# Scores of a cross-attention block: rounded queries and their rest stacked in one stationary tile

## What is computed

```python
x = x + tanh(g_xattn[0]) * xattn(layernorm(x), ctx, ctx, Wq, bq, Wk, bk, Wv, bv, Wo, bo)
x = x + tanh(g_ffn[0]) * ffn(layernorm(x), w_gate, w_up, w_down)

# xattn, with q, k, v = (.. @ W + b) split into 16 heads of 16
scores = einsum('bhld,bhsd->bhls', q, k) * 16 ** -0.5
out = einsum('bhls,bhsd->bhld', softmax(scores), v) @ Wo + bo

# ffn; fp4(t) rounds blocks of 16 to 8 magnitudes times max(|block|) / 6, and back
h = silu(fp4(x) @ fp4(w_gate).T) * (fp4(x) @ fp4(w_up).T)
out = fp4(h) @ fp4(w_down).T
```

## Time and profile before

| | |
|---|---|
| median of 3 runs | 278.96 us (278.86 to 279.12) |
| the profiled execution | 278.86 us, of it the span of the core 277.0 us |
| TensorE busy | 261.6 us, 94% |
| VectorE busy | 242.0 us, 87% |
| ScalarE busy | 165.1 us, 60% |
| GpSimd busy | 129.7 us, 47% |
| granted TensorE clock | full over the whole span |

### The profile page before, as it was taken

How to read it: one execution, slowest core, us unless ns; L and a number is a source line. 1 busy time by engine, 2 the same in 40 slices (tenths; PEclk the granted TensorE clock), 3 DMA queues, 4 the chain that set the end, 5 groups by cost and what they waited for, 6 DMA issues and landing times.

```text
span 277.0 us, 5431 instructions
## 1 busy us (share of the span) xinstructions
PE 261.6 (94%) x1657; PEld 229.2 (83%) x1660; DVE 242.0 (87%) x713; ACT 165.1 (60%) x534; POOL 129.7 (47%) x162
## 2 busy tenths in 40 slices
PE   4999999999999998999999999999999999979795
PEld 2559988999889897999898999999998998757563
DVE  2799999999999998997888889989879999999692
ACT  1438789796765677475665847747576564443421
POOL 1389475823264864641615245354341625543630
PEclk9999999999999999999999999999999999999999
DMA  4993000000000000000000000000000000000001
GB/s 107 311 369 111 1 2 0 0 2 4 2 0 19 2 20 2 20 0 21 1 21 0 0 22 1 19 2 19 0 21 2 22 0 19 2 20 0 19 19 40
DMA packets 9059, 8.64 MB, mean 31 GB/s; under 512 B 1580, under 2 KB 8775, under 8 KB 9031
## 3 DMA queue, kind: packets, MB, share of 16 engines
q1 hardware_dynamic: 7255, 7.50, 8.4%
q10 hardware_dynamic: 1776, 0.79, 1.1%
HBM read 6.19 MB, written 2.10 MB: 30 GB/s over the span
## 4 chain that ended last, share of the span: by engine, by line
PE 46%; issue 21%; POOL 15%; DVE 15%; DMA 2%; SPq 0%; ACT 0%; POOLq 0%; DVEq 0%
PE psT L1963 7%; PE psO L1949 7%; PE psO L1957 7%; POOL ha L1703 4%; POOL hq L1706 4%; PE psG L1935 3%; POOL ha L1714 3%; PE psG L1940 3%; PE psG L1936 3%; PE psO L2018 3%; PE psO L1980 3%; PE psS L1918 2%; PE psS L1915 2%; PE psS L1921 2%; POOL rstd L1675 2%
## 5 line engine op out<-in xcount | busy, mean ns | idle before, releaser
L394 ACT ACTIVATE probs<-psS,negmax 128x77 f32<-128x77 f32 x256 | 59.6, 345 | 4.9 <-DVE negmax L897 4.8
L1957 PE MATMUL psO<-wdT,hT 128*128 128x256 f32 x192 | 44.3, 380 | 1.5 <-ACT hT L445 1.4
L1703 POOL TENSOR_TENSOR ha<-hc,ha 128x704 f32<-128x704 bf16 x15 | 23.2, 1548 | 38.1 <-DVE ha L943 38.1
L1935 PE MATMUL psG<-wgh,xqh 128*128 128x512 f32 (+1 forms) x96 | 38.7, 404 | 2.0 <-DVE h L914 1.5
L1957 PEld LDWEIGHTS psO<-wdT,hT 128*128 128x128 f32 x192 | 35.4, 190 | 6.3 <-issue 1.6
L467 ACT ACTIVATE th<-psG 128x256 f32<-128x256 f32 (+1 forms) x48 | 17.8, 375 | 33.2 <-PE psG L1940 33.1
L1949 PE MATMUL psO<-vblk,pT 128*128 128x51 f32 x320 | 37.5, 271 | 0.0
L421 ACT ACTIVATE pT<-psT 128x512 f32<-128x512 f32 (+1 forms) x48 | 24.6, 530 | 21.5 <-PE psT L1963 21.1
L1949 PEld LDWEIGHTS psO<-vblk,pT 128*128 128x128 f32 x320 | 37.2, 192 | 0.0
L1936 PE MATMUL psG<-wgl,xqh 128*128 128x512 f32 (+1 forms) x96 | 36.0, 375 | 0.0
L897 DVE TENSOR_REDUCE negmax<-psS 128x4 f32<-128x308 f32 x64 | 28.2, 466 | 1.3 <-PE psS L1921 0.8
(11 more groups left out here) (120 smaller groups left out, 609.8 us busy)
## 6 DMA issues: line engine op xcount, KB each, us to landing
out_x<-X SPq DMA_DIRECT2D x16, 128.0 KB, 1.7
X<-in_x SPq DMA_DIRECT2D x2, 512.0 KB, 9.7
wraw<-in_L_ffn_w_down SPq DMA_DIRECT2D x1, 704.0 KB, 9.4
wraw<-in_L_ffn_w_gate ACTq DMA_DIRECT2D x1, 640.0 KB, 9.5
wraw<-in_L_ffn_w_up SPq DMA_DIRECT2D x1, 640.0 KB, 8.4
X<-in_x SPq DMA_DIRECT2D x4, 128.0 KB, 6.5
X<-in_x SPq DMA_DIRECT2D x2, 256.0 KB, 8.8
vblk<-in_vmask SPq DMA_DIRECT2D x2, 255.0 KB, 7.4
```

Source lines behind the costliest of these rows:

```text
L394: ins = act.activation(probs[:, p, hd * S:(hd + 1) * S], psS[g % 2][:, k * S:(k + 1) * S], ACT.Exp, bias=negmax[:, p, hd:hd + 1])
L1703: pool.tensor_tensor(ha[:, p], hc[:, p], ha[:, p], ALU.subtract).then_inc(d_r, 1)
L1935: pe.matmul(o, xqh[:, p, k], wgh[:, k, at:at + w], start=(k == 0), stop=False)
L1957: return pe.matmul(psO[1][:, 0:D], hT[:, p, c * P:(c + 1) * P], wdT[:, c, :], start=(c == first), stop=(c == last))
```

## The change

q and its rest are stacked. The 64 partitions that a group's four heads don't use, zeros in the moving operand until now, get the other part of q. For the groups with `e = g % 2 = 0` the stationary tile `qs[:, p, 0, k]` has the rounded q of those heads in partitions 0 to 63 and their rest in 64 to 127; for `e = 1` the rounded part is in 64 to 127 and the rest in 0 to 63. The keys are doubled: both halves of the moving operand hold the same keys of the group's heads. One matmul with `kh` then gives qh kh + ql kh, one with `kl` gives qh kl + ql kl, so a group has two matmuls of 128 x 308 instead of three.

```
             def scores(n, p, g):
-                k, at = g // 2, (g % 2) * GW
-                if g % 2 == 0:
-                    done(pe, q_hi, KC, n, k + 1)
+                k, e = g // 2, g % 2
+                if g < 2:
+                    done(pe, q_lo, 2, n, e + 1)
...
-                pe.matmul(o, qh[:, p, k], hi, start=True, stop=False)
-                if g % 2 == 0:
-                    done(pe, q_lo, KC, n, k + 1)
-                pe.matmul(o, ql[:, p, k], hi, start=False, stop=False)
+                o, q = psS[e][:, 0:GW], qs[:, p, e, k]
+                pe.matmul(o, q, kh[:, p, k, e * GW:(e + 1) * GW], start=True, stop=False)
...
-                pe.matmul(o, qh[:, p, k], lo, start=False, stop=True).then_inc(s_sc, 1)
+                pe.matmul(o, q, kl[:, p, k, e * GW:(e + 1) * GW], start=False, stop=True).then_inc(s_sc, 1)
```

ScalarE now writes q with its bias as plain floats to `qf`, then copies each half, rounded, into its place in `qs`. VectorE subtracts, from one half of the partitions into the other. The bank is free after `qf` (`q_f` instead of `q_lo` in q_proj and attention_out):

```
             def q_rounded(n, p):
...
+                done(act, q_lo, 2, n - 2)
+                for k in range(KC):
+                    act.activation(qf[:, p, k], psO[0][:, k * P:(k + 1) * P], ACT.Identity,
+                                   bias=bqc[:, k:k + 1]).then_inc(q_f, 1)
                 done(act, s_sc, NG, n - 2)
-                for k in range(KC):
-                    act.activation(qh[:, p, k], psO[0][:, k * P:(k + 1) * P], ACT.Identity,
-                                   bias=bqc[:, k:k + 1]).then_inc(q_hi, 1)
+                done(act, q_f, KC, n)
+                for e in range(2):
+                    act.activation(qs[e * H:(e + 1) * H, p, e], qf[e * H:(e + 1) * H, p], ACT.Copy).then_inc(q_hi, 1)
...
-                    dve.scalar_tensor_tensor(out=ql[:, p, k], in0=psO[0][:, k * P:(k + 1) * P],
-                                             scalar=bqc[:, k:k + 1], in1=qh[:, p, k].bitcast(F32), op0=ALU.add,
-                                             op1=ALU.subtract).then_inc(q_lo, 1)
...
+            def q_rest(n, p):
+
+                for e in range(2):
+                    done(dve, q_hi, 2, n, e + 1)
+                    d = (1 - e) * H
+                    dve.tensor_tensor(qs[d:d + H, p, e], qf[e * H:(e + 1) * H, p],
+                                      qs[e * H:(e + 1) * H, p, e].bitcast(F32), ALU.subtract).then_inc(q_lo, 1)
```

For the doubled keys, ScalarE and VectorE each copy wk once into `wkd` (`key_weights`), so that every 64 output columns stand twice; `keys_proj` has eight matmuls instead of four, and `kT`, `kTh`, `kTl` are twice as large:

```
+            def key_weights():
+
+                dve.wait_ge(l_wk, 16)
+                dve.tensor_copy(wkd[:, :, :, 0], wk[:, :, :].rearrange("p k (g c) -> p k g c", c=H)).then_inc(s_wkd, 1)
...
             def keys_bias():
                 dve.wait_ge(s_kT, 1)
-                dve.wait_ge(l_bk, 16)
+                dve.wait_ge(l_bk, 32)
                 for k in range(KC):
-                    dve.tensor_scalar(kT[:, k], psT[1][:, k * B * S:(k + 1) * B * S], bkc[:, k:k + 1], 0.25, ALU.add,
-                                      ALU.mult).then_inc(s_kTs, 1)
+                    for e in range(2):
+                        dve.tensor_scalar(kT[:, k, e], K_BANKS[k][:, e * B * S:(e + 1) * B * S], bkc[:, k, e:e + 1], 0.25,
+                                          ALU.add, ALU.mult).then_inc(s_kTs, 1)
...
             def keys_proj():
                 pe.wait_ge(s_cTs, 1)
-                pe.wait_ge(l_wk, 16)
+                pe.wait_ge(s_wkd, 2)
```

More of the change, by code:

```diff
@@ L1111, in _ @@
             att_norm(0, 0)
-            q_rest(2, 0)
+            norm_q_apply(3, 1)
+            weights_lo(0)
             maxima(1, 1, 2)
@@ L1203, in _ @@
             h_add(0, 0)
-            x_scale(2)
-            q_rest(6, 0)
-            norm_q_stats(9, 1)
-            norm_q_mean(9, 1)
-            gated(1, 1, 0)
-            gated(1, 1, 1)
-            hidden(1, 1, 0)
-            x1_stats(3, 1)
-            x1_mean(3, 1)
-            h_max(1, 1, 0)
-            x_inv(2)
-            x_a(2)
-            hidden(1, 1, 1)
-            gated(1, 1, 2)
-            hidden(1, 1, 2)
+            gated(1, 1, 0)
+            norm_q_stats(9, 1)
+            hidden(1, 1, 0)
+            x1_mean(3, 1)
+            maxima(6, 0, 0)
+            x_max(2)
+            maxima(6, 0, 1)
+            gated(1, 1, 1)
+            gated(1, 1, 2)
+            norm_q_apply(7, 1)
+            norm_q_mean(9, 1)
+            h_max(1, 1, 0)
+            hidden(1, 1, 1)
+            hidden(1, 1, 2)
+            x_scale(2)
             h_max(1, 1, 1)
@@ L1242, in _ @@
             att_norm(5, 1)
-            q_rest(7, 1)
+            x_max(3)
+            x_scale(3)
+            x_inv(3)
+            maxima(6, 0, 3)
+            gated(2, 0, 0)
+            norm_q_stats(10, 0)
+            norm_q_mean(10, 0)
             x_a(3)
-            norm_q_mean(10, 0)
-            gated(2, 0, 0)
             hidden(2, 0, 0)
             h_max(2, 0, 0)
-            norm_q_stats(11, 1)
             x_add(3)
-            x_sub(3)
+            x1_mean(4, 0)
+            q_rest(7, 1)
@@ L1349, in _ @@
             h_floor(4, 0)
+            x1_mean(7, 1)
             h_add(4, 0)
-            maxima(9, 1, 1)
             maxima(9, 1, 2)
-            q_rest(10, 0)
+            maxima(9, 1, 3)
             gated(5, 1, 0)
@@ L1491, in _ @@
             hidden(9, 1, 0)
-            maxima(13, 1, 3)
+            h_max(9, 1, 0)
+            q_rest(14, 0)
             gated(9, 1, 1)
             hidden(9, 1, 1)
-            h_max(9, 1, 0)
-            h_max(9, 1, 1)
-            gated(9, 1, 2)
-            hidden(9, 1, 2)
-            x_quant(10, 0)
+            x_add(10)
+            x_sub(10)
+            x_quant(10, 0)
+            gated(9, 1, 2)
+            maxima(14, 0, 0)
+            hidden(9, 1, 2)
+            h_max(9, 1, 1)
+            h_max(9, 1, 2)
+            h_scale(9, 1)
+            h_inv(9, 1)
+            x1_sum(12, 0)
+            x1_stats(12, 0)
+            x1_mean(12, 0)
+            residual_out(8)
             x_max(11)
@@ L2207, in _ @@
             hidden_T(1, 1, 1)
-            attention_out(5, 1)
+            scores(7, 1, 0)
+            scores(7, 1, 1)
             xn_T(8, 0)
@@ L2212, in _ @@
             probs_T(6, 0, 2)
-            scores(7, 1, 0)
-            scores(7, 1, 1)
+            q_proj(8, 0)
             x_T(3, 1)
-            q_proj(8, 0)
             values_a(6, 0)
@@ L2254, in _ @@
             probs_T(8, 0, 2)
+            scores(9, 1, 0)
+            scores(9, 1, 1)
             values_a(8, 0)
@@ L2329, in _ @@
             hidden_T(7, 1, 1)
+            scores(13, 1, 0)
             scores(13, 1, 1)
@@ L2335, in _ @@
             scores(13, 1, 2)
+            scores(13, 1, 3)
             q_proj(14, 0)
@@ L2348, in _ @@
             attention_out(12, 0)
+            scores(14, 0, 0)
             xn_T(15, 1)
```

999 lines of the change are left out of this document (497 added, 502 removed).

## The result

The kernel after takes 287.3 us (287.1 to 287.7), the kernel before 279.0 beside it on the same chip: ratio 1.030, 95% interval 1.028 to 1.032. The forecast was 281.0, slower, range 275.0 to 285.0. The direction held; the size did not, and the time lies outside the range.

A forecast was written before the change was run, and what follows sets the result against it. TensorE was taken to bound 100 to 240 us, VectorE with TensorE 20 to 100 us. Span 277.0 + 2.0 start + 4.1 VectorE - 4.0 TensorE = 279.1, plus 1.9 around it: 281.0 us, range 275.0 to 285.0.

The forecast's parts named there:

- The bound: TensorE bounds from 100 to 240 us, VectorE 11% below its limit; from 20 to 100 us both full, VectorE tighter.
- TensorE, -4.0: One of three score matmuls a group removed: 4.3 us gained from 100 to 240 us, 0.3 given back for waits.
- VectorE, q_rest, +0.58 a tile: The subtraction pair crossing partition halves loses its overlap with neighbours, costing 0.58 us more a tile.
- ScalarE, hidden: q_rounded's two added instructions a tile, about 0.7 us, hide as a total because ScalarE is 60% busy.
- That rival: ScalarE becomes the bound early, 40 to 60 us, with 0.6 us left free: +3 on the forecast, 284 us; chance 0.14.
- Start, +2.0: Doubled key projection, waits for copies and more key work on VectorE: between 1.4 and 3.7 us, taken as 2.0.
- The weights_scale calls put ahead of keys(0): At the start, both calls placed there fill VectorE's wait, so less than the full 3.7 us counts.
- Longer path of q, nothing: Project, add bias, round, subtract takes longer, but q_proj runs far ahead of its scores, so no later wait.
- Tail, unchanged: The chain of the last FFN tiles, from 240 us on, counts the same before and after.
- 4.1: VectorE's q_rest cost from 20 to 100 us: 7 tiles at 0.58 us.

The follow-up runs named there:

- the rest on GpSimd: After with values_out(1) early, and GpSimd instead of VectorE computing the rest of q of tiles 2 to 7: 282.1 us, ratio 1.010.
- the rest in the lower half: After with values_out(1) early, q_rest reading and writing only partitions 0 to 63, the rest left out of the scores: 279.6 us, ratio 0.999.
- after with its holes filled: After plus matmuls on zeros in TensorE's three holes of the start (16, ten and ten), nothing else moved: 284.0 us, ratio 1.016.
- keys first: After with values_out(1) early, and instructions reordered to serve the scores first, keys(0) and q_rest(0,0) sooner on VectorE: 286.4 us, ratio 1.025.
- POOL order: After with values_out(1) early, and GpSimd's weights_q(0) moved behind rstd of tile 2, keys_lo(1) and weights_a(1): 288.4 us, ratio 1.034.
- values_out(1) early: After with one ScalarE call, values_out(1), moved directly behind values_out(0), ahead of the first exponentials: 283.4 us, ratio 1.011.
- hole filled: The no holes kernel with 16 instead of eight matmuls on zeros ahead of the first scores: 282.1 us, ratio 1.011.
- The old order: After's functions in the written-out order of the kernel before on all four engines, copies of wk in front: 308.6 us, ratio 1.107.
- the matmul alone: Before without the second of three score matmuls a group; q_rest still runs on VectorE, its result unused: 274.4 us, ratio 0.982.
- with matmuls on zeros: After with values_out(1) early, plus 16 matmuls on zeros behind keys_proj and six ahead of the first scores: 285.7 us, ratio 1.013.
- no holes: The rest on GpSimd kernel plus 12 matmuls on zeros behind keys_proj, eight ahead of the first scores, tile 2's statistics behind keys(0): 283.8 us, ratio 1.013.
- weights early: Keys first and POOL order combined, further with weights_sub(0) ahead of weights_scale(1) and 12 matmuls on zeros behind keys_proj: 289.2 us, ratio 1.036.

## Why the prediction was wrong, step by step

- **The bound.** TensorE from 100 us on: right (137.4 of 140 us busy, and the gain of the matmul taken away alone lies there). From 20 to 100 us I named VectorE, with TensorE full too. How close they are, the rest on GpSimd and the rest in the lower half show: 0.9 and 0.35 us a tile off VectorE gave 1.3 and 1.6 us from tile 2 to 7, and no more.
- **TensorE, -4.0.** Right. Taking the matmul away alone gives 4.8 us from tile 7 to the end (178.0 to 173.2). After gives 1.9 there; 1.6 more is the clock, which falls once more in its profile, to half from 238.8 to 242.2 us (last stretch 64.0 us, and 62.4 in after with its holes filled, keys first and POOL order, where it does not fall), so 3.5.
- **VectorE, q_rest, +0.58 a tile.** Right in mechanism, near in size, too high in what it carries. From the end of the instruction ahead of a pair to the start of the one behind it, an undisturbed pair takes 0.93 us, where before it took 0.43: +0.50. Over tiles 2 to 7 the kernel loses 1.6 us (60.7 against 59.1), where five tiles by 0.58 are 2.9. The Trainium skill (VectorE: DVE Perf Modes, section Two Vector instructions with no wait between them) gives the rule that an instruction whose inputs or output start in another quadrant of partitions than the last ones is held until the earlier ones have finished; this case agrees, since none of the 32 starts before that end, and it shows the price, 31 ns after the end instead of some 80 ns before it. My 0.48 for an instruction with both inputs in SBUF was misread: it is a mean over 16, of which one took 1.49 us beside GpSimd and the median one 0.42. The row already held the price that tile 1's pair was to pay.
- **ScalarE, hidden.** Right as a total: 17.64 of 20 us from 40 to 60, the pair of copies 0.85 us. That rival is out. But its order was not hidden: one call behind the exponentials held TensorE for 2.45 us.
- **Start, +2.0.** This is the step that failed. I had the first scores 3 to 5 us late and let only 2.0 count, on the ground that VectorE is full from 20 us on and only its own lost time carries. With the pairs of tiles 1 and 2 at 0.58 the forecast had 3.2 at tile 2; it comes 9.2 us later, and tile 1 9.3. What the sum had at nothing is idle time of VectorE behind the first maxima: 5.0 us from 30 to 40 us, against 0.2 in before.

  The way from tile 0 to tile 1 takes it apart. It takes 13.6 us in after, 11.5 with values_out(1) early and the clock still fallen, 10.3 with after's holes filled and the clock full, and 8.2 with both (rest on GpSimd, hole filled). So waiting in the chain ScalarE's values_out(1), TensorE, VectorE's maxima, ScalarE's exponentials costs 2.1 us, and the granted clock 3.3 (2.7 by the filled hole): together 5.4 of the 9.3.

  The other 3.9 is VectorE's own work: the two runs with both have tile 1 at 32.9 and 34.1, 3.4 and 4.6 behind before. It can be counted: kT starts at 9.88 instead of 8.37 (1.5), the keys take 1.1 more (kT 0.6, kTl 0.3, the rest kh and kTh), the pairs of q_rest of tiles 0 and 1 take 0.5 and 1.5 more, 1.1 of the latter for the run beside GpSimd. Without the pairs, which the forecast counts elsewhere, that is 2.6, so the 2.0 was a little low and is not the error. The weights_scale calls put ahead of keys(0) hid nothing of it: tile 0 itself comes 5.3 us late. Putting the scores first did not win it back either.
- **Longer path of q, nothing.** Right for the order of after: TensorE waits for a qs once, at the start. The old order shows what the same functions cost without it.
- **Tail, unchanged.** Wrong by 2.8 us (59.6 to 62.4), beside the clock. It belongs to the new order: the matmul alone has 58.9, and the new functions in the old order have 60.0. In the new order tile 15 stands earlier against the last FFN tiles, so the 6.3 us gained from tile 7 to 15 are partly lent; how much of them, I did not separate.

The ledger, read off the ruler: 277.0 + 9.2 (up to tile 2; forecast 3.2) + 1.6 (to tile 7; forecast 2.9) - 1.9 (to the end; forecast 4.0) = 285.9, beside a span of 285.8. No kernel here that computes all of the scores is faster than before: the best median is 282.1. What is left when the clock stays is shown by single runs at a mean clock of 0.999 or more: 280.6 to 281.3 us with values_out(1) early, some 2 us over before, and 282.3 to 284.1 in the order of after. So with a full clock too no run here is faster than before. That the first of these lie at the forecast's 281.0 is luck: its terms were 2.0, 4.1 and -4.0, and none of them is what these runs have.

## What to carry to other kernels

Price the start of a pipeline as a chain over all engines: where one engine is full right behind it, the idle time and delay of the start stay until the end, while a gain in the steady part must be earned tile by tile. Before moving work ahead to fill one engine's wait, look in the order of each other engine for what is queued behind the result that becomes late. And look at the granted clock of the start: a TensorE that is made to wait a little can pay for it again at half speed.

## What the hardware showed that I had not expected

- **The clock falls with short holes, late.** In five of these kernels (values_out(1) early, alone and with matmuls on zeros; no holes; weights early; rest in lower half) TensorE stood idle for 1.0 to 1.9 us, until 21.7 to 24.4 us; 0.7 to 3.0 us later, when it was busy again, the grant was 0.50 for 3.4 to 13.6 us. Holes of 0.39 and of 0.53 us did not do it in their profiles, and one of 1.61 us between two runs of ten matmuls on zeros did not either. But with two matmuls alone the longest hole was 0.47 us, at 18.9, and the clock was at half from 25.7 to 29.1. I can't tell from the length of a hole alone whether it falls.
- **VectorE and GpSimd slow each other down.** q_rest has two inputs in SBUF: 420 ns alone, 1481 in after beside GpSimd and 2044 with keys first, each ending 0.28 us after GpSimd's; kh 1.64 us for its four and 3.69 beside kl; GpSimd's kl 2.75 and up to 4.54. ql of before read one of its inputs from PSUM, and its pair took 0.58 at the same place, with GpSimd's kl beside it. The Trainium skill (SBUF — State Buffer, section Terms) says that the two share one pair of SBUF ports, which one instruction holds whole while the other waits; the numbers here agree. This price of the change, 1.1 us in after (1.93 for the second pair instead of 0.87), was in no term of the sum.
- **Half the partitions save nothing.** A copy of 64x256 on ScalarE takes 417 ns, one of 128x256 420; the subtraction of 64x256 takes 420 ns on VectorE, where a product of 128x256 with both inputs in SBUF (xq) has a median of 424 in after, and 732 on GpSimd, where the addition of 128x256 has a median of 728.
